# Two-layer vision block on one core: router and convolution steps of block two in other places, and every transposed probability copied by ScalarE

## The reference

```python
x = x + L0_conv(ln_c(x))      # 12 heads of 16, each token sees a 7x7 neighbourhood
t = t + L0_ffn(ln_t(t))       # mixture of 32 experts, top 6, capacity 48, and a shared expert
x = x + L1_conv(ln_c(x))      # 12 heads, 16x16 window attention, written as a convolution
t = t + L1_ffn(ln_t(t))       # rms norm, causal attention with rotary positions (12 query heads,
                              # 3 key heads), rms norm, 16 experts, top 2, softmax weights
```

## Time and profile before

| what | value |
|---|---|
| runs | 1195.1, 1191.37, 1196.11 us; median 1195.1 |
| the profiled execution | 1188.06 us |
| its span, first to last instruction | 1186.1 us |
| busy over the span: TensorE, VectorE, ScalarE, GpSimd | 84%, 61%, 42%, 27% |
| granted TensorE clock, mean | 0.954 |
| an image of block two, window product to window product | 58.1 us |

### The profile page before, as it was taken

How to read it: one execution, slowest core, us unless ns; L and a number is a source line. 1 busy time by engine, 2 the same in 40 slices (tenths; PEclk the granted TensorE clock), 3 DMA queues, 4 the chain that set the end, 5 groups by cost and what they waited for, 6 DMA issues and landing times.

```text
span 1186.1 us, 25674 instructions
## 1 busy us (share of the span) xinstructions
PE 1000.1 (84%) x9377; PEld 787.7 (66%) x9398; DVE 726.6 (61%) x2245; ACT 493.7 (42%) x1223; POOL 317.8 (27%) x514
## 2 busy tenths in 40 slices
PE   4799999999998799977788787878786858989991
PEld 3576767776776545476667676767665647989991
DVE  6586776775865334446576867676768685423334
ACT  1453644634625222205465546455555644222220
POOL 0000000000000290607444454454511020433331
PEclk8899999999999889999999999999999989999996
...
DMA packets 68852, 144.04 MB, mean 121 GB/s; under 512 B 4864, under 2 KB 55184, under 8 KB 66592
## 3 DMA queue, kind: packets, MB, share of 16 engines
...
## 4 chain that ended last, share of the span: by engine, by line
PE 50%; DVE 20%; issue 17%; ACT 6%; DMA 3%; POOL 3%; POOLq 0%; DVEq 0%; ACTq 0%; SPq 0%
PE bank L1900 8%; PE bank L2037 5%; PE bank L640 4%; PE bank L592 4%; DVE neg_max L740 4%; PE bank L662 3%; PE bank L704 3%; PE bank L839 3%; PE bank L1928 2%; DVE R L713 2%; PE bank L846 2%; PE bank L615 2%; DMA R<-in_ffn_gu 2%; PE bank L1987 2%; PE bank L670 1%
## 5 line engine op out<-in xcount | busy, mean ns | idle before, releaser
L769 ACT ACTIVATE R<-bank,neg_max 128x128 f32<-128x128 f32 (+2 forms) x576 | 188.1, 398 | 117.9 <-DVE neg_max L740 117.4
L1090 POOL TENSOR_SCALAR R<-cf,ids_rel 128x128 bf16<-128x128 f32 x256 | 166.1, 666 | 38.2 <-PE bank L2017 37.8
L640 PE MATMUL bank<-cf,R 128*128 128x128 f32 x864 | 138.5, 285 | 27.8 <-ACT R L778 23.2
L740 DVE TENSOR_REDUCE neg_max<-bank 128x2 f32<-128x352 f32 (+2 forms) x216 | 130.3, 610 | 47.1 <-PE bank L615 41.5
L640 PEld LDWEIGHTS bank<-cf,R 128*128 128x128 f32 x864 | 99.3, 145 | 48.2 <-ACT R L769 32.9
L1042 POOL TENSOR_TENSOR rstd<-mean_var,cf 128x2 f32<-128x2 f32 x24 | 4.6, 194 | 406.0 <-DVE mean_var L904 405.7
L592 PE MATMUL bank<-cb,R 128*128 128x128 bf16 x1008 | 76.7, 239 | 28.0 <-DVE R L569 28.0
L792 ACT ACTIVATE R<-bank 128x1024 bf16<-128x1024 bf16 x72 | 71.8, 1021 | 61.6 <-PE bank L592 60.7
L1900 PE MATMUL bank<-R 64*116 64x256 f32 (+1 forms) x512 | 97.3, 398 | 0.0
L592 PEld LDWEIGHTS bank<-cb,R 128*128 128x128 bf16 x1008 | 68.5, 108 | 35.2 <-DVE R L569 24.6
L1900 PEld LDWEIGHTS bank<-R 64*116 64x116 f32 (+1 forms) x512 | 65.2, 180 | 26.0 <-issue 16.4
...
## 6 DMA issues: line engine op xcount, KB each, us to landing
...
```

The lines of the kernel that those rows point to most:

```text
L640: ins = nc.tensor.transpose(PT[u % 2][:, at + g * P:at + (g + 1) * P], probs[:, u % 3, g * kw + c0:g * kw + c0 + P], ident)
L740: nc.vector.tensor_reduce(neg_max[:, u % 4, 0:g], score_bank(a, u)[:, 0:g * kw].rearrange("p (g k) -> p g k", g=g), AX, ALU.max, negate=Tr ...
L769: ins = nc.scalar.activation(probs[:, u % 3, g * kw:(g + 1) * kw], score_bank(a, u)[:, g * kw:(g + 1) * kw], ACT.Exp, bias=neg_max[:, u % ...
L1090: ins = nc.gpsimd.tensor_scalar(comb_s[i % 2][:, t, j, :], cst("iota_tok"), ids_rel[:, j:j + 1], None, ALU.is_equal)
```

## The change

It has these parts:

- `Attention` gets a flag `shared`; only block one's attention has it. WINDOW and CAUSAL have ScalarE copy every unit's transposed probabilities, behind exponential u the copy of unit u-2.
- `sorted_rows` is cut in two: `ranked` reads the ranks (one VectorE instruction, raises `c_ranked`), the rest stands with `weights` at the end of the window half, before the first maximum of the causal half. TensorE's first combination products wait for `c_ranked`, and stand behind the transposes of unit 0; the products are dealt out 12 at a time.
- window half on VectorE: rotations one place earlier, so too the steps of `split_qk`; `m_rows` from place 2 to place 8; `combine` at 7.
- `m_head` moves on TensorE from the window half to the causal half (place 1), its copy on ScalarE to place 2; the logits from place 1 to 3; router steps on VectorE from 1, 4, 5, 6, 7 to 4, 6, 7, 7, 8, 9.
- causal half: the three convolution steps move one unit on, on TensorE (2, 3, 4 for 1, 2, 3) and VectorE alike.
- the first q/k transposes of the causal attention stand behind the second transposes of sums, not before.
- GpSimd: the scatter behind the two roots of the image, the one-hot tiles of tile 0 before `w_root`.

The core of the diff:

```diff
@@ Attention
-        self.by_dve = (self.n + 1) // 2
-        self.by_act = self.n // 2
+        self.by_dve = (self.n + 1) // 2 if shared else 0
+        self.by_act = self.n - self.by_dve
+    def copied(self, u):
+        if not self.by_dve:
+            return "pta", u + 1
+        return "pta" if u % 2 else "ptd", u // 2 + 1
@@ attention_dve
-                if 2 <= u < a.n + 2 and u % 2 == 0:
+                if 2 <= u < a.n + 2 and a.copied(u - 2)[0] == "ptd":
                     copy_pt(u - 2)
@@ attention_act
-                if u >= 2 and u % 2 == 1:
+                if u >= 2 and a.copied(u - 2)[0] == "pta":
                     v = u - 2
@@ GpSimd
                 if i >= 1:
                     c_root("h", i - 1)
-                if i >= 2:
-                    c_scatter(i - 2)
+                if i >= 0 and i + 3 < B:
+                    c_onehot(i + 3, 0)
                 if 0 <= i < B - 2:
                     w_root(i + 2)
...
                     c_root("u", i + 1)
+                if i >= 2:
+                    c_scatter(i - 2)
@@ ScalarE, c_causal
                 if 1 <= i < B - 1:
-                    before[4] = lambda: router(i - 1)
+                    before[2] = lambda: m_head(i - 1)
+                    before[5] = lambda: router(i - 1)
@@ VectorE
+            def ranked(i):
+                dve.wait_ge(s("c_rank"), i + 1)
+                nc.vector.tensor_tensor(slot_g[:, :, :], two(RANKS),
+                                        cst("regions").unsqueeze(1).to_broadcast([P, 2, E1]), ALU.add)\
+                    .then_inc(s("c_ranked"), 1)
@@ VectorE, c_window
                 if i >= 2:
-                    between[1].append(lambda: weights(i - 2))
-                    between[1].append(lambda: sorted_rows(i - 2))
-                if i >= 1:
-                    between[2].append(lambda: m_rows(i - 1))
+                    between[0].append(lambda: ranked(i - 2))
                 if i + 2 < B:
-                    between[6 if i else 3].append(lambda: combine(i + 2))
-                    between[8 if i else 5].append(lambda: w_norm(i + 2))
+                    between[7 if i else 3].append(lambda: combine(i + 2))
...
-                at = (2, 3, 4, 5, 6, 7, 8, 8) if i else (5, 6, 6, 6, 7, 7, 8, 8)
+                at = (1, 2, 3, 4, 5, 6, 7, 7) if i else (5, 6, 6, 6, 7, 7, 8, 8)
...
+                if i and i + 2 < B:
+                    between[8].append(lambda: w_norm(i + 2))
+                if i >= 1:
+                    between[8].append(lambda: m_rows(i - 1))
...
                 run(copies)
+                if i >= 2:
+                    weights(i - 2)
+                    sorted_rows(i - 2)
@@ VectorE, c_causal
-                        between[1].append(lambda: conv_qk_dve(dve, WINDOW, brow, i + 2, (0,)))
-                        between[2].append(lambda: conv_qk_dve(dve, WINDOW, brow, i + 2, (1,)))
-                        between[3].append(lambda: conv_v_dve(dve, WINDOW, brow, i + 2))
-                    between[2].append(lambda: normed(i + 1))
+                        between[2].append(lambda: conv_qk_dve(dve, WINDOW, brow, i + 2, (0,)))
+                        between[3].append(lambda: conv_qk_dve(dve, WINDOW, brow, i + 2, (1,)))
+                        between[4].append(lambda: conv_v_dve(dve, WINDOW, brow, i + 2))
+                    between[1].append(lambda: normed(i + 1))
...
-                    between[1].append(lambda: highest_logit(m))
-                    between[4].append(lambda: probabilities(m))
-                    between[5].append(highest)
-                    between[6].append(strike)
-                    between[7].append(lambda: masks(m))
-                    between[7].append(lambda: earlier(m))
-                for k, n in ((4, 0), (5, 1), (6, 2), (8, 3), (9, 4), (10, 5)):
+                    between[4].append(lambda: highest_logit(m))
+                    between[6].append(lambda: probabilities(m))
+                    between[7].append(highest)
+                    between[7].append(strike)
+                    between[8].append(lambda: masks(m))
+                    between[9].append(lambda: earlier(m))
+                for k, n in ((5, 0), (5, 1), (6, 2), (8, 3), (9, 4), (10, 5)):
@@ TensorE, c_window
-                        pe.wait_ge(s("c_slots"), i - 1)
-                    c_comb(i + 2, 0, 5)
+                        pe.wait_ge(s("c_ranked"), i - 1)
+                    c_comb(i + 2, 0, 4)
...
-                        extra[2] = first_unit
+                        extra[(2, "transposed")] = first_unit
...
-                if i >= 1:
-                    extra[(8, "transposed")] = lambda: m_head(i - 1)
-                extra["weighted"] = lambda: transpose_qk(pe, CAUSAL, i, n1=1)
-                extra["turned"] = lambda: transpose_qk(pe, CAUSAL, i, n0=1, n1=3)
+                extra["turned"] = lambda: transpose_qk(pe, CAUSAL, i, n1=3)
@@ TensorE, c_causal
-                    extra[1] = conv_0
-                    extra[2] = conv_1
-                    extra[3] = conv_2
+                    extra[2] = conv_0
+                    extra[3] = conv_1
+                    extra[4] = conv_2
...
-                    extra[(1, "transposed")] = lambda: logits(i - 1)
-                    extra[(10, "transposed")] = lambda: ranks(i - 1)
+                    extra[1] = lambda: m_head(i - 1)
+                    extra[(3, "transposed")] = lambda: logits(i - 1)
+                    extra[(11, "transposed")] = lambda: ranks(i - 1)
```

35 lines of the change are left out of this document (18 added, 17 removed).

## The result

| | median us | runs | ratio to before, 95% interval |
|---|---|---|---|
| before | 1194.5 | 1191.4 to 1196.1 | |
| changed | 1166.0 | 1164.5 to 1168.5 | 0.9763 [0.9738, 0.9787] |

What follows compares the result with a forecast made beforehand. No engine is full; engines wait in turn, and waits ending last at TensorE, plus its slow clock after them, bound block two. Gains of 13.2 + 2.1 + 10.0 + 5 = 30.3 us gave 1165 us, range 1150 to 1185.

Steps and rivals of the forecast that it cites:

- The wait for `slots`, -1.25: Window half, images with slots: TensorE needs only the ranks read, so its 1.25 us wait before the combination products goes.
- The copy of unit 0 behind exponential 2, +0.8: Window half: ScalarE's copy, walked through to 742.8 us, delays the first weighted sum; a new wait costs 0.8 us.
- Maxima start later: Sign that the forecast is wrong: maxima starting later in relation to product L709 than before; no size given.
- Statistics, -0.56: Window half: the router's transposes move to the causal half, so their 0.56 us wait for statistics goes.
- Parts and normalisation, -0.9: Window half: the 1.96 us wait for q/k parts goes; waiting about 1.1 us for the second tile's normalisation replaces it.
- The clock, -1.4: Window half: without the long wait, the slow-clock stretch behind it goes too, 3.4 us becoming 2.0.
- The copies, -2.4: Causal half: copies moved to ScalarE free VectorE of 0.6 us each, four of five counting: 2.4 us gained.
- the order, +0.4: Causal half, moved steps: convolution wait covered -0.8, weights and sorted rows +0.7, router's transposes and their copy +0.5 us.
- The rest of block two, -5 forecast: First two and last window images, first and last two causal ones: 24 copies leave VectorE, a third counted, 5 us.
- Half of it: Rival, chance 0.19: ScalarE's chain holds the weighted sums, slow stretches stay; 8 to 18 us gained, 1177 to 1187.
- More: Rival, chance 0.11: both slow-clock stretches go, 1.4 us more per causal half; 38 to 48 us gained, about 1152.
- Slower: Rival, chance 0.08: in-order queues delay maximum 2 and the causal half's first maximum and residual sum; 12 us slower, 1207.

Runs made afterwards that it cites:

- e3_ranked: Kernel before with the ranks read by their own instruction ahead of maximum 1 and TensorE waiting for that alone: 1182.6 us, ratio 0.9915.
- e5_head: Changed kernel with the copy of unit 0 moved ahead of exponential 2 on ScalarE in each window image: 1160.7 us, ratio 0.9750.
- e4_parts: Changed kernel with the last three steps of the q and k split again behind the combination's sum and w_norm: 1171.2 us, ratio 0.9818.
- e1_copies: Kernel before, its order kept, with ScalarE making all copies of transposed probabilities in block two: 1175.5 us, ratio 0.9862.
- e2_order: Changed kernel with copies shared between VectorE and ScalarE as before, all new places kept: 1181.7 us, ratio 0.9901.
- e6_late: Changed kernel with copies shared again only in the last window image and last two causal ones: 1165.6 us, ratio 0.9788.

## Why the prediction was right, point by point

The rows that the prediction calls the neighbourhood attention's products are, in block two, those of the window attention, and 645.24 and 877.52 are starts, not ends; the 58.1 us stand.

**Window half, -3.3 forecast, -3.2 measured** (four halves, 12.9 of 13.2 us; image 1: 2.0 of 2.1). The terms:

1. *The wait for `slots`, -1.25.* Right; the ranks alone gave 1.4 at equal clock (e3_ranked).
2. *The copy of unit 0 behind exponential 2, +0.8.* Right in place and way, 0.8 to 1.35 measured (it was to be under 1). The walk had the copy at 742.2 us, 9.5 behind its product; it came 9.6 behind. The move in e5_head shows the cause. Maximum 2 itself started 7.9 us behind the product, where it had been 6.4, as the walk had it. "Maxima start later" was named as a sign of being wrong; it came true, and did not make the half longer. By the Trainium skill, "PSUM — Partial Sum Buffer", section "Engine vs sequencer instructions", the queues of ScalarE and VectorE are strict FIFO: the trace agrees, since a copy that needed nothing of exponential 2 started 3.4 us later behind it than ahead of it.
3. *Statistics, -0.56.* The wait went, but 0.61 for the gathering took its place. What the half gained are the router's transposes, which left it.
4. *Parts and normalisation, -0.9.* 1.96 became 0.71; putting the steps back costs 0.7 to 1.0 at equal clock (e4_parts).
5. *The clock, -1.4.* 1.2, seen alone in e3_ranked. The size held; its condition, that the long wait has to go, is not shown: e1_copies ran its window halves at 1.00 with a wait of 1.53 us left, and e3_ranked three of its four with slots with 1.84 to 1.95. Terms 2 to 4 together were forecast at -0.66; at equal clock they gave 26.07 - 25.48 = 0.6.

**Causal half, -2.0 forecast, -2.4 measured** (five, 12.1 of 10 us). Here the sum was near and its terms were not, which is luck. *The copies, -2.4*, gave 1.4 alone (2.1 in image 1, at clock 1.00); *the order, +0.4* (convolution -0.8, sorting +0.7, router's transposes +0.5), cost 0.9 alone. Of the convolution's 0.81 us of waiting 0.52 are left. Together the two gave 2.7 in images 2 to 4, and 0.5 of that is the slow clock, which the forecast put at nothing here. The two are no separate terms. I read it so: both lengthen or shorten one queue, and what copies take off VectorE is worth more when the order has filled it.

**The rest of block two, -5 forecast, 0 measured.** This is the step that failed: *"loses 24 copies of 0.6 us from VectorE. I let a third count"*. Four of its stretches can be followed.

- The first one gained 0.9 us, within what it varies by among the kernels here (31.3 to 33.4 us).
- The causal half of image 0 took 26.4 us before and 26.5 after. The copies alone made it 25.2 (e1_copies). The changed order ran it in 25.4 where the clock stood at 1.00 (e5_head); in the changed kernel it fell to 0.94, and that took the gain of 1 us back.
- The late window half gained 1.1 us, with a new wait of 3.64 us for ScalarE's copy in it.
- The causal half of image 6 lost 1.65. TensorE idles 5.6 us in it instead of 4.6: the wait for the gathering of tile 0 has doubled, as the two rows below show (before, then changed), and waits of 0.33 us for VectorE's statistics and of 0.41 and 0.38 for ScalarE's copies are new. The 0.33 stands in e2_order too, the 0.41 in e1_copies: each edit alone makes the half 1.2 us longer.

```profile
942.06 0.55 PE L670 MATMUL bank<-cf,R 128*128 128x128 f32 x3 [0.46 <-ACT R L758]
...
914.90 0.55 PE L675 MATMUL bank<-cf,R 128*128 128x128 f32 x3 [0.99 <-ACT R L763]
```

So a third of the copies' length is no price. The same copies were worth 1.2 us where TensorE had waited for them, and less than nothing where it then waited for ScalarE; sharing them again in the late halves brought nothing either (e6_late). The middle stretch fell short of the 30 us by 3, and the median by 1.5. That it came so near is partly luck: the causal halves gave 2 more than forecast, and 1.6 us of the median's gain lie outside the middle stretch, where two profiles of one kernel differ by more than that.

**GpSimd, 0.** No wait of TensorE in block two ends with GpSimd after the change. Its old order was not tried on its own. Per image VectorE is busy 4.6 us less and ScalarE 4.0 more, where 5 and 5 were named.

**The rivals.** *Half of it* was right in one point: ScalarE's chain does end most of TensorE's waits now, though none is over 1.9 us in images 1 to 5. *More* had its condition met in most halves and not its price: both slow stretches went in images 1 to 4. In the window half that is the 1.2 us of term 5; in the causal half it is 0.5 us where 1.4 were asked, and 0.05 in the order before, since TensorE there waits for other engines at either level. The rule of the Trainium skill that stood beside it, "TensorE: Matmul & The Clock Gate", section "HAM oscillation — how this bites in real kernels", is that recurring idle gaps drop the array to its half rate and that closing them keeps it warm. The trace agrees as far as the level goes in those images: with the long gaps the low stretches went. In the causal half of image 0 it does not: before, TensorE had four waits of 0.76 to 1.25 us and no fall; in the changed kernel it has two, of 0.98 and 1.86, and the clock fell. The rule doesn't give the time, and e3_ranked has the same gap of 1.95 us once with the fall and once without, so what else decides stays open. *Slower* had the right queue: the order alone costs 0.6 to 2.3 us in each of the five causal halves (e2_order), but the window half's 2.9 us outweigh it even without the copies.
